# The last attention's keys turned beside the state-space scan, and their norms read as rows from DRAM

## The chip, the cores and the metric

One core of one Trainium2 chip runs the whole program. The core has a matrix engine (TensorE, PE; its weight loads are PEld), a vector engine (VectorE, DVE), a scalar engine (ScalarE, ACT), GpSimd (POOL) and SyncE (SP), which issues nearly all transfers. Each engine takes its own instructions in order and waits for the others only by semaphores. The metric is the device time of one execution in microseconds (us), lower is better.

## The reference

Eight layers stand one after the other on `x` of 4 x 256 tokens with 256 features, each `x = x + layer(layernorm(x))`. Two matter here, the first and the seventh. Shapes are those that reach them (the weights' own setup sizes are others).

```python
# first layer, a selective state-space layer on the context (4 x 256 tokens, 128 features)
x = einsum('bld,ed->bel', ctx, in_proj_w);  x = silu(causal_conv(x, conv_w) + conv_b)
dt_low, Bm, Cm = split(einsum('bdl,ed->bel', x, x_proj_w))       # 8, 16, 16 rows
dt = softplus(dt_proj(dt_low) + dt_proj_b);  A = -exp(A_log)     # 256 x 16
for each token:  state = state * exp(dt * A) + (dt * x) * Bm;  y = sum_n state_n * Cm_n
out = (y + D * x) * silu(z)                                      # z: the normed x

# seventh layer, cross-attention, 16 heads of 128, keys and values from the same context
q = (h @ Wq).reshape(B, 256, 16, 128);  k = (ctx @ Wk)...;  v = (ctx @ Wv)...
q = q * rsqrt(mean(q*q) + 1e-5) * gq
k = k * rsqrt(mean(k*k) + 1e-5) * gk
attn = softmax(einsum('bqhd,bkhd->bhqk', q, k) / sqrt(128))
out = einsum('bhqk,bkhd->bqhd', attn, v).reshape(B, 256, 2048) @ Wo
```

The keys and values of the seventh layer depend on the context alone, so they can be made at any time.

## The kernel before

**The state-space layer (`mamba`).** The 16 states are 16 iterations n. The 256 channels are two halves j of 128 partitions, and a row holds all 1024 tokens. For each state DVE multiplies `dBu` for both halves (L757, L758), scans half 0 (L753), multiplies it by the row of C (L764) and scans half 1 (L753); POOL does the product with C of half 1 (L796). PE spreads a row of B and then a row of C over the partitions into banks 4 and 5 (`spread`, L561) and adds the products into banks 0 to 3 (`add`, L566). ACT makes `exp(dt*A)` (`decay`, L661) and copies the spread row of C out of PSUM (L671). DVE's next state can start when the next row of B is spread (`m_b`), its product with C when that copy is done (`m_c_copied`).

**Keys and values made beside it.** 32 rounds r make the keys and values of the last attention: `kv_round` (PE, 4 products, L503, eight instructions in the trace) into banks 6 and 7, `kv_out` (ACT, L603) into one of four buffers `staged`, and SP stores it to DRAM. 24 rounds stand in the scan: one at the end of every iteration, and a second one ahead of it in each even iteration (`EXTRA`). 16 rounds make keys; `squares` (ACT, L612) sums their squares in the iteration behind. A round waits until the last user of banks 6 and 7 was copied out (`m_kv_copied`). Behind the scan DVE takes the 1/rms of all keys (L195 to L210, `g.k_rs`), between the two output steps `gated_out(0)` and `gated_out(1)` (L770, L773).

**The last attention (`attn4`).** Eight turns t, one for each pair of heads. A turn has 11 slots written out by hand. In slots 0 to 7 a unit (head, sequence) gets its scores (PE, L2717), maximum (DVE, L2868), exponential (ACT, L2804), division (DVE, L2876), transpose of the weights (PE, L2727), its copy (ACT, L2812), the product with V (PE, L2739) and its copy (DVE, L2882), each a slot or more behind the last; the output projection (PE, L2765) follows. The jobs for the next turn stand in the table `JOBS`, by slot, with the PSUM bank: projection of q (PE, L2687, copied by DVE, L2861, squares by ACT, L2784), its transposes (`qt`: PE, L2695, ACT, L2793), and `kt`, the same for k. Before that DVE multiplies a head of k by its 1/rms (L2851, `keys`). A turn -1 has only jobs. POOL takes the 1/rms of q (L107 to L114) from the squares, and DVE needs it (L2886) before the first maximum.

## Time and profile before

| | |
|---|---|
| median of 3 runs | 1496.79 us (1494.49 to 1501.44) |
| profiled execution | 1492.03 us, its span 1490.3 us |
| busy: PE, DVE, ACT, POOL | 87%, 71%, 48%, 14% of the span |
| scan, about 48 to 186 us | iterations of 8.6 us |
| last attention, about 1023 to 1320 us | turns of 36.1 us |

The profile is of one execution. Times in its rows are us from the start of the span. An engine's idle time before an instruction is put down to what released it. PE instructions overlap: eight of one kind start at even distance and the last one's end lies some 0.17 us behind the next one's start. Register, semaphore and branch instructions are not counted as busy.

### The profile page before, as it was taken

To read this page: it belongs to the slowest core of one execution; us is meant where nothing else is said; L and a number is where in the kernel's file an instruction comes from. 1 tells how busy PE (TensorE), PEld (TensorE's weight loads), DVE (VectorE), ACT (ScalarE), POOL (GpSimd) and SP (SyncE) were. 2 spreads that over 40 slices of the span, in tenths; PEclk is the share of its full clock that TensorE was granted. 3 is DMA by queue.
4 is the path that set the end of the run, shared out by engine and by line. 5 is a ranking of instruction groups with operands and counts; after the bars stand their busy time and mean duration, and the time that the engine had idled before them with its cause. 6 is when DMAs were issued, how large, how long until landed. Compare 5 with 4: busy or idle time off the path is not lost.

```text
span 1490.3 us, 20843 instructions
## 1 busy us (share of the span) xinstructions
PE 1302.3 (87%) x6612; PEld 908.7 (61%) x6620; DVE 1052.7 (71%) x2211; ACT 720.0 (48%) x1836; POOL 216.0 (14%) x227
## 2 busy tenths in 40 slices
PE   7788869986998667999998699985999999889998
PEld 4444445652333344676676588984888888774555
DVE  7999987888996787777876623225666666668565
ACT  5788813443775655555544112223666666633111
POOL 0132220000000002211220173111111111201000
PEclk9899979996999769999999699997999999989999
DMA  5122240015420100010004197845322222101230
GB/s 189 72 98 99 85 190 1 1 29 87 78 46 15 70 1 1 1 37 1 36 1 133 56 344 284 305 182 167 106 70 70 70 70 70 35 1 47 77 91 29
DMA packets 77776, 124.61 MB, mean 84 GB/s; under 512 B 44965, under 2 KB 56430, under 8 KB 72352
## 3 DMA queue, kind: packets, MB, share of 16 engines
q1 hardware_dynamic: 75824, 119.37, 24.6%
q0 software_dynamic: 1872, 4.22, 0.7%
q8 instruction: 44, 0.72, 0.2%
q14 instruction: 36, 0.29, 0.1%
HBM read 88.28 MB, written 26.24 MB: 77 GB/s over the span
## 4 chain that ended last, share of the span: by engine, by line
PE 68%; DVE 19%; issue 7%; ACT 4%; DMA 2%; DVEq 1%; SPq 0%; POOL 0%; ACTq 0%; POOLq 0%
PE psum L2397 5%; DVE roomA L753 5%; PE psum L3181 5%; PE psum L873 4%; PE psum L1978 4%; PE psum L2739 4%; PE psum L2687 4%; PE psum L2717 3%; PE psum L2020 3%; PE psum L2765 3%; PE psum L2408 3%; PE psum L3191 3%; PE psum L2010 2%; PE psum L907 2%; DVE roomB L1535 2%
## 5 line engine op out<-in xcount | busy, mean ns | idle before, releaser
L2804 ACT ACTIVATE roomA<-psum,roomA 128x256 f32<-128x256 f32 x128 | 70.9, 559 | 92.7 <-DVE roomA L2870 92.4
L2066 ACT ACTIVATE roomA<-psum,roomA 128x128 f32<-128x128 f32 (+1 forms) x128 | 53.2, 426 | 88.5 <-DVE roomA L2141 88.3
L1535 DVE TENSOR_REDUCE roomB<-psum 128x2 f32<-128x512 f32 x128 | 82.1, 686 | 9.7 <-PE psum L1374 8.4
L2539 DVE SCALAR_TENSOR_TENSOR roomA<-roomA,psum 128x512 f32<-128x512 f32 x23 | 15.9, 689 | 98.6 <-ACT roomA L2444 98.6
L1978 PE MATMUL psum<-own,roomB 128*128 128x512 f32 x160 | 75.0, 594 | 3.4 <-DVE roomA L2133 2.1
L1941 POOL TENSOR_TENSOR roomA<-roomA 128x512 f32<-128x512 f32 x40 | 50.8, 1272 | 176.9 <-DVE roomA L2134 176.9
L3181 PE MATMUL psum<-roomA,roomB 128*112 128x512 f32 (+1 forms) x168 | 74.8, 593 | 0.3 <-DVE roomA L3409 0.3
L2739 PE MATMUL psum<-roomA 128*128 128x256 f32 x256 | 68.3, 389 | 6.0 <-DVE roomA L2882 4.4
L753 DVE TENSOR_TENSOR_SCAN roomA<-roomA 128x1024 f32<-128x1024 f32 x32 | 73.1, 2284 | 0.0
L2717 PE MATMUL psum<-roomA 128*128 128x256 f32 x256 | 65.6, 379 | 1.7 <-ACT roomA L2804 1.7
L873 PE MATMUL psum<-own,roomB 128*128 128x512 f32 x144 | 66.6, 607 | 0.0
L1374 PE MATMUL psum<-roomB,roomA 48*128 48x256 bf16 x256 | 51.9, 301 | 16.7 <-DVE roomB L1535 9.4
L3289 ACT ACTIVATE roomA<-psum 48x512 f32<-48x512 f32 (+1 forms) x32 | 19.0, 594 | 97.8 <-PE psum L3181 97.8
L503 PE MATMUL psum<-roomB,own 128*128 128x256 f32 x256 | 65.3, 403 | 0.0
L503 PEld LDWEIGHTS psum<-roomB,own 128*128 128x128 f32 x256 | 51.6, 203 | 21.5 <-issue 13.0
L2687 PE MATMUL psum<-roomB,own 128*128 128x256 f32 x256 | 62.7, 390 | 1.6 <-DVE own L288 0.8
L566 PE MATMUL psum<-roomA,own 128*128 128x512 f32 x128 | 60.4, 593 | 2.5 <-DVE roomA L764 1.3
L796 POOL TENSOR_TENSOR roomA<-roomA 128x1024 f32<-128x1024 f32 x16 | 37.9, 2366 | 146.4 <-DVE roomA L753 146.4
L2020 PE MATMUL psum<-roomB,roomA 128*128 128x256 f32 x256 | 58.2, 379 | 0.8 <-DVE roomA L2158 0.8
L2450 ACT COPY roomA<-psum 128x256 f32<-128x256 f32 x23 | 8.6, 373 | 100.3 <-PE psum L2408 92.8
L2765 PE MATMUL psum<-roomB,roomA 128*128 128x256 f32 x256 | 56.7, 378 | 0.0
L2687 PEld LDWEIGHTS psum<-roomB,own 128*128 128x128 f32 x256 | 49.9, 196 | 9.6 <-issue 1.1
(526 smaller groups left out, 3331.8 us busy)
## 6 DMA issues: line engine op xcount, KB each, us to landing
roomB<-m_w_dram SPq DMA_DIRECT2D x12, 1536.0 KB
roomA<-m_w_dram SPq DMA_DIRECT2D x11, 1536.0 KB
a_kv_ready<-roomB SPq DMA_DIRECT2D x32, 512.0 KB, 3.1
roomA<-a_kv_ready SPq DMA_DIRECT2D x8, 1024.0 KB, 4.8
roomA<-a_kv_ready SPq DMA_DIRECT2D x16, 512.0 KB, 4.2
roomB<-a_w_dram SPq DMA_DIRECT2D x4, 1280.0 KB, 5.8
roomB<-f_w_dram SPq DMA_DIRECT2D x8, 624.0 KB, 3.9
roomA<-f_c_rows SPq DMA_DIRECT2D x6, 512.0 KB, 3.9
```

The costliest lines, as they stand in the source:

```text
L503: ins = pe.matmul(g.ps[:, at * HALF + i * 2 * P:at * HALF + (i + 1) * 2 * P], g.CT[:, t * P:(t + 1) * P], w_kv[:, place_of[r] // 2 * 2 + k ...
L753: dve.tensor_tensor_scan(h[:, j, :], dA[:, j, :], dBu[j], 0.0, ALU.mult, ALU.add).then_inc(s["m_scanned"], 1)
L873: ins = pe.matmul(g.bank(4 + 2 * (k % 2) + w), w_up[:, kt, e, w * HID:(w + 1) * HID], g.XT[:, kt, half * HALF:(half + 1) * HALF], start=(k ...
L1535: dve.tensor_reduce(maxneg[:, hp // 8, :, m, hp % 8], g.bank(m).rearrange("p (q k) -> p q k", k=S), AX.X, ALU.max, negate=True).then_inc(s ...
L1978: ins = pe.matmul(bank, w, g.XT[:, kt, half * HALF:(half + 1) * HALF], start=(kt == 0), stop=(kt == KD - 1))
L2020: ins = pe.matmul(g.bank(OUT)[:, r * D:(r + 1) * D], OT[:, n % 2, h, r * P:(r + 1) * P], wo[:, h, :], start=(h == 0), stop=(h == HQ - 1))
L2397: ins = pe.matmul(g.bank(4 + 2 * (b % 2) + w)[:, f * P:(f + 1) * P], parts(b)[0][:, kt, at:at + P], xT[:, b % 2, kt, :], start=(kt == 0), ...
L2687: ins = pe.matmul(g.bank(bank)[:, i * 2 * P:(i + 1) * 2 * P], g.XT[:, kt, (2 * j + i) * P:(2 * j + i + 1) * P], w_q[:, kt, :], start=(kt = ...
L2717: ins = pe.matmul(g.bank(2 + n % 2)[:, qt * S:(qt + 1) * S], qT[:, q, i * P:(i + 1) * P], kT[:, q, b * S:(b + 1) * S], start=True, stop=True)
L2739: ins = pe.matmul(g.bank(5, S), V[:, q, (2 * b + kt) * P:(2 * b + kt + 1) * P], PT[:, n % 2, kt, :], start=(kt == 0), stop=(kt == 1))
L2765: ins = pe.matmul(g.bank(OB[k])[:, r * D:(r + 1) * D], OT[:, q, i * P:(i + 1) * P], w_o[:, q, :], start=(q == 0), stop=(q == 1))
L3181: ins = pe.matmul(g.bank(bank, rows=m), w[:, kt, at:at + m], xg[:, n % 2, kt, half * HALF:(half + 1) * HALF], start=(kt == 0), stop=(kt == ...
```

## The change

In `mamba` each keys round is turned in the iteration behind it: `turn_keys` (PE) transposes the eight 128x128 blocks from `staged` into banks 6 and 7, `keys_out` (ACT) copies them to one of two buffers `turned`, and SP stores that instead of `staged`. The list `uses` numbers the rounds and turns in the order in which they take banks 6 and 7. In the attention no k is transposed: DVE multiplies the loaded keys by the gain and by `k_scale`, a row of 1/rms that a broadcast transfer puts on all partitions, into `kT` itself. Those rows come from `a4_scales` in DRAM, written once at the start of the attention from a transpose of `g.k_rs`. `JOBS` loses its four `kt` entries, and `keys` stands in slots 5 and 9 (0 and 2 in turn -1) where it stood in 0 and 5.

```diff
@@ mamba
+    keys_in = [[r for r in rs if kind_of[r] == 0] for rs in in_loop]
+    uses = [("round", r) for r in range(EARLY + MIDDLE)]
+    for n in range(NS):
+        uses += [("turn", r) for r in (keys_in[n - 1] if n else ())] + [("round", r) for r in in_loop[n]]
@@ mamba, tensor
+            before = uses[:uses.index(("round", r))]
+            earlier = [k for k, (what, q) in enumerate(before) if (6 if what == "turn" else pair_of[q]) == at]
             if earlier:
                 pe.wait_ge(s["m_kv_copied"], earlier[-1] + 1)
+        def turn_keys(r):
+            pe.wait_ge(s["m_kv_copied"], uses.index(("turn", r)))
+            for q in range(2):
+                for i in range(4):
+                    ins = pe.transpose(g.bank(6 + q)[:, i * P:(i + 1) * P], staged[:, r % 4, q, i * P:(i + 1) * P], g.ident)
+            ins.then_inc(s["m_kv_psum"], 1)
                 add(1, s["m_added1"])
+            for r in keys_in[n - 1] if n else ():
+                turn_keys(r)
             for r in in_loop[n][:-1]:
                 kv_round(r)
             pe.wait_ge(s["m_hc0"], n + 2)
@@ mamba, scalar
-            for r in in_loop[n - 1] if n else ():
-                if kind_of[r] == 0:
-                    squares(r)
+            for r in keys_in[n - 1] if n else ():
+                squares(r)
+                keys_out(r)
             for r in in_loop[n][:-1]:
                 kv_out(r)
@@ attn4
-    JOBS = {0: (("q", 0, 0),), 1: (("q", 1, 1),), 2: (("q", 2, 6),), 3: (("q", 3, 0),), 4: (("kt", 0, 1),), 5: (("kt", 1, 6),),
-            6: (("qt", 0, 0),), 7: (("qt", 1, 1),), 8: (("kt", 2, 6), ("kt", 3, 0)), 9: (("qt", 2, 1), ("qt", 3, 6))}
+    JOBS = {0: (("q", 0, 0),), 1: (("q", 1, 1),), 2: (("q", 2, 6),), 3: (("q", 3, 0),),
+            5: (("qt", 0, 1),), 6: (("qt", 1, 6),), 8: (("qt", 2, 0),), 9: (("qt", 3, 1),)}
@@ attn4, sync
         def keys(n):
             load(k_in, ready(n, 0), "a4_k_in")
+            load(k_scale.rearrange("p q t -> p (q t)"), scales[bass.ds(n, 1), :].to_broadcast([P, 2 * TOK]), "a4_k_in")
+        sp.wait_ge(s["a4_rows"], 1)
+        sp.wait_ge(s["a4_small"], 16)
+        load(scales.rearrange("n (q i t) -> (n q i) t", q=2, i=NT), rows, "a4_small")
+        sp.wait_ge(s["a4_small"], 32)
         keys(0)
@@ attn4, vector
-            dve.wait_ge(s["a4_k_in"], n * 16 + 16)
-            if units:
-                dve.wait_ge(s["a4_kt_psum"], t * 4 + 2 * q + 2)
-            dve.tensor_tensor(norm_k[:, q], k_in[:, q, :].rearrange("p (i c) -> p i c", c=P),
-                              g.k_rs[:, bass.ds(n * 2 + q, 1), :].rearrange("p a i -> p (a i)").unsqueeze(2).to_broadcast([P, NT, P]),
-                              ALU.mult).then_inc(s["a4_kn"], 1)
+            dve.wait_ge(s["a4_k_in"], n * 32 + 32)
+            dve.scalar_tensor_tensor(kT[:, q, :], k_in[:, q, :], gains[:, 1:2], k_scale[:, q, :], ALU.mult, ALU.mult)\
+               .then_inc(s["a4_kn"], 1)
-                if jobs and slot in (0, 5):
-                    keys(t, slot // 5, units)
+                if jobs and slot in ((5, 9) if units else (0, 2)):
+                    keys(t, int(slot in (2, 9)), units)
```

Two new steps stand ahead of the attention's norm: PE transposes `g.k_rs` and ACT copies it to `rows`. POOL waits once for the last stores before it fills V in the second attention. The line numbers of the changed kernel are some 8 to 31 higher.

On PE, in iteration 2 of the scan (even), these rows stood from the spread of C to the next spread of C: C (L561), `add(1)` (L566), the extra round (L503), the next B (L561), `add(0)` (L566), the last round (L503).

```order
L561 MATMUL psum<-roomA 128x512 x2
L566 MATMUL psum<-roomA,own 128x512 x2
L503 MATMUL psum<-roomB,own 128x256 x4
L561 MATMUL psum<-roomA 128x512 x2
L566 MATMUL psum<-roomA,own 128x512 x2
L503 MATMUL psum<-roomB,own 128x256 x4
```

The same place now (L576 is `spread`, L581 `add`, L511 the round, L519 `turn_keys`):

```order
L576 MATMUL psum<-roomA 128x512 x2
L581 MATMUL psum<-roomA,own 128x512 x2
L519 MATMUL psum<-own,roomB 128x128 x8
L511 MATMUL psum<-roomB,own 128x256 x4
L576 MATMUL psum<-roomA 128x512 x2
L581 MATMUL psum<-roomA,own 128x512 x2
L511 MATMUL psum<-roomB,own 128x256 x4
```

The transposes stand ahead of the extra round, and the spread of the next B stands behind both.

On ACT the same iteration had: the two decays (L661), the copy of the last round of the iteration before (L603), the copy of C (L671), the squares (L612), the copy of the extra round (L603), and the decays.

```order
L661 ACTIVATE roomA<-roomA 128x4x255 x2
L603 COPY roomB<-psum 128x1024
L671 COPY roomA<-psum 128x1024
L612 ACTIVATE roomB,own<-roomB 128x128 x8
L603 COPY roomB<-psum 128x1024
L661 ACTIVATE roomA<-roomA 128x4x255 x2
```

It now has (L685 decay, L620 a round's copy, L695 the copy of C, L636 squares, L627 `keys_out`):

```order
L685 ACTIVATE roomA<-roomA 128x4x255 x2
L620 COPY roomB<-psum 128x1024
L695 COPY roomA<-psum 128x1024
L636 ACTIVATE roomB,own<-roomB 128x128 x8
L627 COPY roomA<-psum 128x1024
L620 COPY roomB<-psum 128x1024
L685 ACTIVATE roomA<-roomA 128x4x255 x2
```

The copy of the transposes stands behind the squares and ahead of the copy of the extra round.

On SP, where the attention starts, behind the loads of the layer before (`m_sums`), the keys (128x2048) and the two halves of V followed:

```order
L2324 DMA roomA<-m_sums 128x2x256 x8
L2614 DMA roomA<-a_kv_ready 128x2048
L2614 DMA roomA<-a_kv_ready 128x1024 x2
L2614 DMA roomB<-a_q_dram 128x512
```

Now:

```order
L2350 DMA roomA<-m_sums 128x2x256 x8
L2642 DMA a_scales<-roomA 128x128
L2642 DMA roomA<-a_kv_ready 128x2048
L2642 DMA roomA<-a_scales 128x2048
L2642 DMA roomA<-a_kv_ready 128x1024 x2
L2642 DMA roomB<-a_q_dram 128x512
```

A store, which SP waits for, stands ahead of the keys, and the load of the scales between the keys and V.

## Rows read from the trace of the kernel before

**Rows 1.** Timeline of DVE, scan, even iteration: start us, duration us, engine, line, instruction [idle before <-releaser]

```profile
100.03 1.22 DVE L757 TENSOR_TENSOR roomA<-roomA,psum 128x1024 f32<-128x1024 f32 x1 [0.40 <-DVE roomA L753]
102.30 2.28 DVE L753 TENSOR_TENSOR_SCAN roomA<-roomA 128x1024 f32<-128x1024 f32 x1
104.80 1.22 DVE L764 TENSOR_TENSOR roomA<-roomA,psum 128x1024 f32<-128x1024 f32 x1 [0.21 <-DVE roomA L753]
...
108.62 1.22 DVE L757 TENSOR_TENSOR roomA<-roomA,psum 128x1024 f32<-128x1024 f32 x1 [0.40 <-DVE roomA L753]
```

**Rows 2.** Timeline of PE, the same iteration

```profile
102.44 0.60 PE L561 MATMUL psum<-roomA 96*128 96x512 bf16 x2 [0.90 <-DVE roomA L758]
...
104.60 1.89 PE L503 MATMUL psum<-roomB,own 128*128 128x256 f32 x8
106.33 0.60 PE L561 MATMUL psum<-roomA 96*128 96x512 bf16 x2
106.76 1.88 PE L566 MATMUL psum<-roomA,own 128*128 128x512 f32 x4
```

**Rows 3.** Timeline of ACT, the same iteration and the next

```profile
103.08 1.01 ACT L671 COPY roomA<-psum 128x1024 f32<-128x1024 f32 x1 [0.49 <-PE psum L561]
...
106.53 1.01 ACT L603 COPY roomB<-psum 128x1024 f32<-128x1024 f32 x1
107.44 2.18 ACT L661 ACTIVATE roomA<-roomA 128x1020 f32<-128x1020 f32 x2
...
111.67 1.01 ACT L671 COPY roomA<-psum 128x1024 f32<-128x1024 f32 x1 [0.25 <-PE psum L561]
```

**Rows 4.** Timeline of DVE and PE behind the last scan

```profile
185.71 1.28 DVE L770 SCALAR_TENSOR_TENSOR roomA<-roomA,roomB,psum 128x1024 f32<-128x1024 f32 x1 [0.22 <-DVE roomA L753]
187.03 2.21 DVE L773 SCALAR_TENSOR_TENSOR roomA<-own,roomA 128x1024 f32<-128x1024 f32 x1
...
193.28 1.22 DVE L773 SCALAR_TENSOR_TENSOR roomA<-own,roomA 128x1024 f32<-128x1024 f32 x1
...
190.03 1.04 PE L592 MATMUL psum<-own,roomA 128*128 128x128 f32 x8
```

**Rows 5.** Windows of the attention: stretch, its us, busy us by engine, PEclk, DMA share, GB/s

```profile
1034.00:1040.00 6.00, 3.67 (x27) 2.65 (x26) 1.82 (x2) 5.91 (x28) 1.67 (x2) 1.00 0.60 195
1113.00:1149.10 36.10, 35.48 (x194) 30.82 (x193) 23.35 (x59) 22.66 (x80) 4.89 (x7) 1.00 0.22 73
1126.34:1134.05 7.71, 7.62 (x47) 6.73 (x46) 7.46 (x20) 6.73 (x25) 3.04 (x2) 1.00 0.12 29
```

**Rows 6.** The chain that ended last, within one turn: start us, us, what

```profile
1131.51 0.44 PE psum L2695 x4
...
1138.90 0.66 PE psum L2695 x4
...
1140.90 0.44 DVE roomA L2882
```

**Rows 7.** Timeline of DVE, the same turn, slot 7

```profile
1134.50 0.69 DVE L2868 TENSOR_REDUCE roomA<-psum 128x2 f32<-128x512 f32 x1 [0.44 <-PE psum L2717]
```

**Rows 8.** Timeline of SP, DVE and PE where the attention starts

```profile
1023.15 1.30 SPq L2614 DMA_DIRECT2D roomA<-a_kv_ready  x3
1030.40 1.22 DVE L2851 TENSOR_TENSOR roomA<-roomA,own 128x1024 f32<-128x1024 f32 x1
...
1043.07 0.18 DVE L2886 TENSOR_SCALAR roomA<-roomA 128x16 f32<-128x16 f32 x1 [6.94 <-POOLq L2839]
...
1046.11 1.02 PE L2717 MATMUL psum<-roomA 128*128 128x256 f32 x4
```

**Rows 9.** DMA issues at the attention's start and in all: operation, count, KB each, us to landing

```profile
roomA<-a_kv_ready SPq DMA_DIRECT2D x2, 1024.0 KB, 4.9
...
roomA<-a_kv_ready SPq DMA_DIRECT2D x2, 512.0 KB, 6.8
...
roomA<-m_steps_dram SPq DMA_DIRECT2D x1, 96.5 KB, 2.0
```

More of the change, by code:

```diff
@@ L462, in mamba @@
     place_of = [(values if kind_of[r] else keys).index(r) for r in range(32)]
+    keys_in = [[r for r in rs if kind_of[r] == 0] for rs in in_loop]
+    assert not keys_in[-1] and min(keys) >= EARLY + MIDDLE
+    uses = [("round", r) for r in range(EARLY + MIDDLE)]
+    for n in range(NS):
+        uses += [("turn", r) for r in (keys_in[n - 1] if n else ())] + [("round", r) for r in in_loop[n]]
     xpad = ra.take(E2, B, S + TAPS - 1)
@@ L470, in mamba @@
     A = ra.take(E2 * NS)
+    turned = ra.take(2, 2, HALF)
     dA, h = e, th
@@ L482, in sync @@
         for r in range(32):
-            sp.wait_ge(s["m_kv_copied"], r + 1)
-            sp.dma_start(g.kv[place_of[r] // 2, kind_of[r], :, :, (place_of[r] % 2) * HALF:(place_of[r] % 2 + 1) * HALF], staged[:, r % 4])\
+            sp.wait_ge(s["m_kv_copied"], uses.index(("round" if kind_of[r] else "turn", r)) + 1)
+            sp.dma_start(g.kv[place_of[r] // 2, kind_of[r], :, :, (place_of[r] % 2) * HALF:(place_of[r] % 2 + 1) * HALF],
+                         staged[:, r % 4] if kind_of[r] else turned[:, place_of[r] % 2])\
               .then_inc(s[f"m_kv_stored{r % 4}"], 16)
@@ L495, in kv_round @@
             at = pair_of[r]
-            earlier = [k for k in range(r) if pair_of[k] == at]
+            before = uses[:uses.index(("round", r))]
+            earlier = [k for k, (what, q) in enumerate(before) if (6 if what == "turn" else pair_of[q]) == at]
             if earlier:
@@ L598, in kv_out @@
         def kv_out(r):
-            act.wait_ge(s["m_kv_psum"], r + 1)
+            act.wait_ge(s["m_kv_psum"], uses.index(("round", r)) + 1)
             if r >= 4:
@@ L603, in kv_out, with keys_out @@
             act.copy(staged[:, r % 4].rearrange("p q (i c) -> p q i c", i=4), src).then_inc(s["m_kv_copied"], 1)
+        def keys_out(r):
+            act.wait_ge(s["m_kv_psum"], uses.index(("turn", r)) + 1)
+            if place_of[r] >= 2:
+                last = keys[place_of[r] - 2]
+                act.wait_ge(s[f"m_kv_stored{last % 4}"], 16 * (last // 4) + 16)
+            act.copy(turned[:, place_of[r] % 2], g.ps[:, 6 * HALF:8 * HALF].rearrange("p (q t) -> p q t", q=2)).then_inc(s["m_kv_copied"], 1)
         def squares(r):
             pair, half = divmod(place_of[r], 2)
-            act.wait_ge(s["m_kv_copied"], r + 1)
+            act.wait_ge(s["m_kv_copied"], uses.index(("round", r)) + 1)
             if place_of[r]:
@@ L1099, in constants @@
         pool.wait_ge(s["f0_made"], 5)
+        for q in range(4):
+            pool.wait_ge(s[f"m_kv_stored{q}"], 8 * 16)
         pool.memset(k.V[:, :, :, HD:], 1.0).then_inc(s["a1_ones"], 1)
@@ L2596, in attn4 @@
     room.at = 0
-    norm_k, raw_q = room.take(2, NT, P), room.take(2, NT, P)
+    raw_q = room.take(2, NT, P)
     kT, qT, V, OT = (room.take(2, TOK) for _ in range(4))
@@ L2603, in attn4 @@
     ta, tb, consts = room.take(2, NT), room.take(2, NT), room.take(3, 2, NT)
-    k_in = room.take(2, TOK)
+    k_in, k_scale = room.take(2, TOK), room.take(2, TOK)
+    rows = room.take(P)
+    scales = g.nc.dram_tensor("a4_scales", (H // 2, 2 * TOK), F32).ap()
     w_q, w_o, gains = g.a4_wq, g.a4_wo, g.a4_gains
-    JOBS = {0: (("q", 0, 0),), 1: (("q", 1, 1),), 2: (("q", 2, 6),), 3: (("q", 3, 0),), 4: (("kt", 0, 1),), 5: (("kt", 1, 6),),
-            6: (("qt", 0, 0),), 7: (("qt", 1, 1),), 8: (("kt", 2, 6), ("kt", 3, 0)), 9: (("qt", 2, 1), ("qt", 3, 6))}
+    JOBS = {0: (("q", 0, 0),), 1: (("q", 1, 1),), 2: (("q", 2, 6),), 3: (("q", 3, 0),),
+            5: (("qt", 0, 1),), 6: (("qt", 1, 6),), 8: (("qt", 2, 0),), 9: (("qt", 3, 1),)}
     SLOTS = 11
@@ L2690, in job @@
             q, half = j // 2, j % 2
-            if what == "kt" and half == 0:
-                pe.wait_ge(s["a4_kn"], n * 2 + q + 1)
-            src = norm_k if what == "kt" else raw_q
             for i in range(4):
-                ins = pe.transpose(g.bank(bank)[:, i * P:(i + 1) * P], src[:, q, 4 * half + i, :], g.ident)
+                ins = pe.transpose(g.bank(bank)[:, i * P:(i + 1) * P], raw_q[:, q, 4 * half + i, :], g.ident)
         ins.then_inc(s[f"a4_{what}_psum"], 1)
@@ L2791, in job @@
                     act.wait_ge(s["a4_scores"], t * 8 + 4 * q + 4)
-                dst, gain = (kT, 1) if what == "kt" else (qT, 0)
-                act.activation(dst[:, q, half * HALF:(half + 1) * HALF], g.bank(bank), ACT.Copy, scale=gains[:, gain:gain + 1])\
+                act.activation(qT[:, q, half * HALF:(half + 1) * HALF], g.bank(bank), ACT.Copy, scale=gains[:, 0:1])\
                    .then_inc(s[f"a4_{what}"], 1)
@@ L2919, in added, with turn_scales, scales_in @@
         dve.sem_inc(s["layer_done"], 1)
+    def turn_scales(pe):
+        pe.transpose(g.bank(0, P), g.k_rs.rearrange("p h i -> p (h i)"), g.ident).then_inc(s["a4_rows_psum"], 1)
+    def scales_in(act):
+        act.wait_ge(s["a4_rows_psum"], 1)
+        act.copy(rows, g.bank(0, P)).then_inc(s["a4_rows"], 1)
     def credits(dve):
+        dve.wait_ge(s["a4_small"], 16)
         dve.sem_inc(s["a4_rs_used"], 1)
```

21 lines of the change are left out of this document (9 added, 12 removed).

## The prediction

> **What bounds the kernel now.** I read the chain that ended last first: DVE carries it through the scan, PE through the last attention. Then the timelines of the two places that the change touches.
>
> *The scan.* DVE's two first multiplies of successive states start at 100.03 and 108.62, 8.59 us apart, and DVE idles only 0.40 and 0.21 us between [rows 1]. DVE is the bound, the others fit around it, and what counts is how late PE and ACT may hand over. PE spreads the next B at 106.33, done at 106.93, 1.69 us before DVE takes it [rows 1, 2]. ACT copies C at 103.08 to 104.09, and DVE needs it at 104.80: 0.71 us to spare [rows 1, 3]; in the odd iteration that follows the copy ends at 112.68, and DVE's product starts at 104.80 + 8.58 = 113.38: 0.70 us to spare.
>
> *The last attention.* One turn is 36.10 us, PE 35.48 of it busy, at granted clock 1.00 [rows 5]. So PE bounds the turn, but not with everything else idle: from 1126.34 to 1134.05 (slots 4 to 6) DVE is busy 7.46 of 7.71 us, without an idle time of its own [rows 5], and only before 1134.50 does it wait, 0.44 us [rows 7].
>
> **The change part by part: the scan.** Added are 16 turnings. One is eight transposes on PE, 1.04 us [rows 4], its place in line 0.87, and one ACT copy of 1024 columns, 1.01 us [rows 3]. The cover is DVE's 8.6 us; a plain count says they fit. They do not fit in an even iteration, because all of it passes through banks 6 and 7 one after the other. I place the new instructions in the rows:
>
> 1. The transposes start where the extra round did, 104.60 [rows 2], and end 105.64.
> 2. Their copy stands on ACT behind the squares, which end at 106.53 (there the extra copy starts now) [rows 3]. It runs to 107.54.
> 3. The extra round waits for that copy: 107.57 instead of 104.60. It takes 1.89 us, 1.73 until the next may start: 109.30.
> 4. Behind it in PE's line is the next B: 109.30 + 0.60 = 109.90, and DVE, ready at 108.62, starts at about 109.94. **Loss 1.32 us.**
> 5. The extra copy runs 109.5 to 110.5, the decays (2.18 us) follow to 112.65. On PE `add(0)` follows B to 111.4, then the last round to 113.3; ACT copies it to 114.35 and then copies C, to 115.35. DVE would take C at 113.38 + 1.32 = 114.70, so it waits until 115.40. **Loss 0.70 us** in the odd iteration, which has no extra round and loses nothing more.
>
> A pair costs 2.03 us. Iteration 0 has no keys behind it; iterations 2 to 13 are six pairs, 12.2 us; iteration 14 gives 1.32. **13.5 us** until iteration 15 starts (at 177.31 before, by the same 8.59 step from 100.03).
>
> Iteration 15 has two keys rounds to turn (those of 14) and PE's `add(0)` behind both turnings. From its start: C copied at 5.4 (step 5's delay), squares 2.4 and copy 1.0 to 8.8; second transposes to 9.7 in line; `add(0)` 1.88 us, to 11.6. `gated_out(0)` needs it. Before it started at 185.71 [rows 4], 8.40 after the iteration's start; now 11.65: 3.25 later. But its second multiply took 2.21 us where the same form later takes 1.22 [rows 4], beside POOL's last product, which now is long done: 0.99 back. The second squares and all else are done before DVE asks. **2.3 us.** The scan's sum: 13.5 + 2.3 = **+15.8 us**. Bounds: every duration is one of a row, so I allow 14 to 17.5.
>
> The stores to DRAM are of the same size and number, an iteration later; the wait that is added to POOL is met long before.
>
> **The turn of the attention.** PE loses 16 transposes, 4 x 0.44 = 1.74 us [rows 6], and a wait of 0.22 on an ACT copy between them (0.66 where others have 0.44). Upper bound of the gain: 1.96 a turn. What of it arrives:
>
> - In the slots, `kt` leaves slots 4, 5 and 8 (twice) and the `qt` of slots 6, 7 and 9 move up: slots 4, 7, 8 and 9 lose 0.44 each. Ahead of slot 7's maximum that is one 0.44, and DVE, whose own work stays (the keys' multiply stays in slot 5; I take its new form at the same 1.22 us, which both forms of 1024 columns have in rows 4 and 8), has just 0.44 of idle there [rows 7]. Played forward from the rows, PE then waits 0.2 us more for DVE's copy of unit 2, and 0.23 arrives.
> - Slots 7 to 9 lose 1.31 + 0.22. There exponentials and copies stand back to back on ACT, and the products of units 4 and 5 wait 0.44 and 0.42 for their copies: 0.67 remains.
> - The keys' multiply of slot 9 stands before DVE's copy that PE already waits for at 1140.90 [rows 6]. Between that copy and the one before are 1.75 us of PE work (two groups of four transposes, one product), DVE needs 0.42 + 1.22: it just fits, and the 0.44 stays.
>
> I take **0.9 us a turn**, seven turns have jobs beside units: **-6.3 us**. Bounds: 0.4 (more of the softmax chain) to 1.96, so -2.8 to -13.7.
>
> **The attention's start.** The keys' load was issued at 1023.15, landed 4.9 us later, and DVE took them at 1030.40, when the norm let it [rows 8, 9]. Now a store of 64 KB stands first and SP waits for it; the 96.5 KB load has 2.0 us to landing [rows 9], so I take 2.0. Behind it the scales, 1 MB, stand where V's two halves stood, and those had 6.8 us from issue to landing, the last of them 7.2 after the first issue. 1023.15 + 2.0 + 7.2 = 1032.4: the multiply starts 2.0 us late. Back come 0.6 us, since ACT has no `kt` copy ahead of the last squares. All that follows (q copies, squares, POOL's root, L2886 at 1043.07 [rows 8]) comes some 1.4 us later; PE's third scores at 1046.11 had 0.5 us of room after the exponential. **+1.0 us.** Bounds: -1.2 if the loads are hidden (then the ACT saving counts), +3.5 if a row read by all 128 partitions is slow.
>
> **Sum.** +15.8 - 6.3 + 1.0 = **+10.5 us**, on the profiled 1492.0: 1502.5. That execution was 4.8 us below the median of the runs, 1496.8, so the median becomes 1507.3; I give **1507**.
>
> **A rule weighed.** In the stretch from 1034 to 1040 PE did little but transposes, 3.67 of 6.00 us busy, and the clock granted was 1.00 [rows 5]. The Trainium skill, "TensorE: Matmul & The Clock Gate", Part 4 (PE-mode transpose), says that transposes do not count as busy for the clock. By that rule the scan's PE, a larger share of it transposes and with a wait of 2 us in every second iteration, could fall to the granted clock 0.5, which is 1.2 GHz; the row speaks against it.
>
> **The rivals.**
>
> - *Full PE saving* (13 in 100). The attention is PE-bound to the end and gives 1.96 a turn: 15.8 - 13.7 + 1.0 = +3.1, 1500. For it: PE 35.48 of 36.10. Against: DVE without idle in slots 4 to 6.
> - *The extra round does not hold the spread* (9 in 100, half of them with the full saving). The one point that decides is step 4: B has 1.69 us to spare and loses 2.97. If transposes and copy cost 1.3 us less than placed, the pairs cost nothing, and +2.3 + 1.0 remain: with -6.3, 1494; with -13.7, **1486, faster**. Against: all the durations are of rows.
> - *The start is worse and the turns give little* (13 in 100): 15.8 + 3.5 - 2.8 = +16.5, 1513. The scales' broadcast is the one transfer with no like in the trace.
> - *PE's clock falls in the scan* (2 in 100). A pair needs some 15.4 us of PE (four spreads at 0.43, four adds and three rounds at 1.73, two turnings at 0.87, less fill) of its 17.2 now; at half clock near 31. Seven times 12: +80 us.
> - *As worked out* (63 in 100): 1507, its own range 1503 to 1511.
>
> The range, 8 in 10: **1500 to 1514**, from the full saving to the bad start. What a measurement here can tell from no change is about 0.5%, 7.5 us, so slower begins at 1504.3. Slower: the forecast less a twelfth, the bad start, the clock: **0.73**. Same: the full saving, half of the second rival and the rest of the forecast: **0.22**. Faster: **0.05**.
>
> **What the changed profile would show.** Step 3: in even iterations PE's extra round starts near 7.5 us after DVE's first multiply (4.57 now). Step 4: DVE idles about 1.7 us before that multiply every second time, released by PE's spread; step 5: 0.9 us before its product with C, released by ACT's copy. Tail: the first multiply of the output (L770 before) starts some 2.8 us behind the last scan, not 0.2. Attention: turns of 35.2 us, PE with new waits of 0.3 to 0.5 us in slots 6 to 8. Start: the first keys' multiply near 2 us later relative to the norm. It is wrong if the scan's iterations stay at 8.6 us, or the turns are at 34.2.

## The result, and the profile after

The change makes the kernel 0.8% slower, little but clear of the noise: 1509.70 us (median of 6 runs, 1508.19 to 1514.77) against 1498.93 us (6 runs), ratio 1.0083, 95% interval 1.0060 to 1.0106. By the ratio that is +12.4 us, 9 to 16; the two medians by themselves are 10.8 us apart. The prediction was 1507 in 1500 to 1514, or +10.5 us.

The profiled executions stand further apart, 1514.77 to 1492.03: before's lay 7 us below its median, after's 5 above. So I compare section by section, on starts of rows. `rs_now` is DVE's first instruction of a turn, which takes the 1/rms of q.

| section | before | after | difference | predicted |
|---|---|---|---|---|
| scan, first multiply to that of iteration 15 | 128.83 | 141.82 | +13.0 | +13.5 |
| from there to the layer's first add on DVE | 17.94 | 21.52 | +3.6 | +2.3 |
| first feed-forward layer (not touched): from that add to the next layer's norm (L251) | 130.36 | 132.17 | +1.8 | 0 |
| attention: last add of the layer ahead to the first `rs_now` (L2886, now L2909) | 20.5 | 23.6 | +3.1 | +1.0 |
| seven steps from `rs_now` to `rs_now` | 253.81 | 247.84 | -6.0 | -6.3 |

The rest of the profiled difference, some 7 us, lies in layers that the change does not touch. They differ as much between two executions of one program: a kernel below that is the kernel before up to 1022 us has one such layer 8.5 us longer.

*Scan.* Timeline of the changed kernel, iterations 6 (even) and 7, which are those of the rows before (start, length, line; idle time ahead and its releaser in brackets). DVE first, answering to [rows 1]:

```profile
104.74 1.22 DVE L781 TENSOR_TENSOR roomA<-roomA,psum 128x1024 f32<-128x1024 f32 x1 [0.40 <-DVE roomA L777]
114.56 1.22 DVE L781 TENSOR_TENSOR roomA<-roomA,psum 128x1024 f32<-128x1024 f32 x1 [1.63 <-PE psum L576]
120.05 1.22 DVE L788 TENSOR_TENSOR roomA<-roomA,psum 128x1024 f32<-128x1024 f32 x1 [0.94 <-ACT roomA L695]
123.87 1.22 DVE L781 TENSOR_TENSOR roomA<-roomA,psum 128x1024 f32<-128x1024 f32 x1 [0.40 <-DVE roomA L777]
```

PE there, answering to [rows 2] (L519 transposes, L511 a round, L576 a spread):

```profile
109.31 1.04 PE L519 MATMUL psum<-own,roomB 128*128 128x128 f32 x8
112.09 1.99 PE L511 MATMUL psum<-roomB,own 128*128 128x256 f32 x8 [1.75 <-ACT roomA L627]
113.92 0.60 PE L576 MATMUL psum<-roomA 96*128 96x512 bf16 x2
```

ACT there, the turned copy and the extra round's, answering to [rows 3]:

```profile
111.04 0.99 ACT L627 COPY roomA<-psum 128x1024 f32<-128x1024 f32 x1
114.12 1.01 ACT L620 COPY roomB<-psum 128x1024 f32<-128x1024 f32 x1 [2.08 <-PE psum L511]
```

Steps 1 to 5 in order: transposes end 5.6 us after the first multiply, their copy starts behind the squares at 6.3, the extra round at 7.35 (predicted 7.5), DVE waits 1.63 us for B (predicted 1.7) and in the odd iteration 0.94 for C (predicted 0.9; 0.21 of it stands in every iteration). The iterations last 9.82 and 9.31 us, a pair 19.13; before, 17.17.

*Tail.* PE and DVE of iteration 15, answering to [rows 4], then the windows there (us, busy time and count of each engine; granted clock third from the end):

```profile
199.74 1.55 PE L519 MATMUL psum<-own,roomB 128*128 128x128 f32 x8 [2.22 <-ACT roomA L627]
201.09 3.15 PE L581 MATMUL psum<-roomA,own 128*128 128x512 f32 x4
```

```profile
204.28 1.28 DVE L794 SCALAR_TENSOR_TENSOR roomA<-roomA,roomB,psum 128x1024 f32<-128x1024 f32 x1 [4.28 <-PE psum L581]
205.59 1.22 DVE L797 SCALAR_TENSOR_TENSOR roomA<-own,roomA 128x1024 f32<-128x1024 f32 x1
```

```profile
199.00:201.00 2.00, 1.26 (x8) 1.26 (x9) 1.00 (x1) 2.00 (x11) 0.69 (x1) 0.81 0.08 25
201.00:203.00 2.00, 2.00 (x5) 0.96 (x4) 0.00 (x0) 1.93 (x9) 1.67 (x1) 0.50 0.64 246
```

The second turning waits 2.22 us for the first copy; the granted clock falls to 0.50 (1.2 GHz), and `add(0)`, 1.88 us elsewhere, takes 3.15. The second output step is back at 1.22 us, as the prediction had it. Three kernels below have the same scan: two of them read the same tail, +3.6, and the third keeps the clock and reads +1.9.

*Start of the attention.* DVE, answering to [rows 8], and the transfers' issues (KB each, us to landing), answering to [rows 9]:

```profile
1055.05 0.69 DVE L288 COPY own<-psum 128x512 f32<-128x512 f32 x1 [3.90 <-PE psum L304]
1057.92 1.28 DVE L2875 SCALAR_TENSOR_TENSOR roomA<-roomA,roomB 128x1024 f32<-128x1024 f32 x1 [2.18 <-DMA roomA<-a_scales]
1059.12 0.68 DVE L2884 COPY roomA<-psum 128x512 f32<-128x512 f32 x1
1070.64 0.18 DVE L2909 TENSOR_SCALAR roomA<-roomA 128x16 f32<-128x16 f32 x1 [6.76 <-POOLq L2865]
```

```profile
roomA<-a_kv_ready SPq DMA_DIRECT2D x1, 1024.0 KB, 4.8
roomA<-a_scales SPq DMA_DIRECT2D x1, 1024.0 KB, 8.2
```

DVE starts the multiply 0.14 us behind the landing of the scales. ACT's first squares of q and, four instructions later, those of the second copy of q:

```profile
1059.89 0.31 ACT L2811 ACTIVATE roomA<-roomA 128x128 f32<-128x128 f32 x1 [4.70 <-DVE roomA L2884]
1061.63 0.31 ACT L2811 ACTIVATE roomA<-roomA 128x128 f32<-128x128 f32 x1 [0.46 <-DVE roomA L2884]
```

Seven kernels below keep this start. In their executions and this one the section is 22.3 to 24.1 us, 1.8 to 3.6 longer than before, so +3.1 is one draw out of these. From the start of the multiply to `rs_now` it is 12.7 us in all eight and in the kernel before, so what differs is when the scales land.

*Turns.* One turn's window, answering to [rows 5], and PE's waits in it, which answer to [rows 6]:

```profile
1139.59:1174.59 35.00, 34.03 (x178) 29.14 (x177) 23.39 (x59) 20.61 (x76) 5.13 (x7) 1.00 0.29 105
```

```profile
1159.74 1.13 PE L2766 MATMUL psum<-roomA 128*128 128x256 f32 x4 [0.23 <-ACT roomA L2838]
1161.92 1.12 PE L2766 MATMUL psum<-roomA 128*128 128x256 f32 x4 [0.18 <-ACT roomA L2838]
1165.30 1.13 PE L2766 MATMUL psum<-roomA 128*128 128x256 f32 x4 [0.52 <-DVE roomA L2905]
```

A steady turn is 35.00 us instead of 36.10: 1.10 arrives. The first step gives 1.46, but the seventh is 0.99 us longer than before. There one pair of DVE's divisions takes 4.41 us, the others 0.61 to 0.69:

```profile
1301.58 4.41 DVE L2899 TENSOR_SCALAR roomA<-roomA 128x256 f32<-128x256 f32 x2
```

The stall is there in the kernel before too (4.32 us), and with the attention of either version; the seventh step varies from 36.8 to 40.9 us over all kernels. It is no doing of the change.

### The profile page after: what moved, and what is told of

It reads as the page before. It is cut to its first block, busy times and chain, and to the rows that moved or that the text cites. A ratio compares the mean times of both kernels' runs of the same rounds, so it can differ in the third digit from the quotient of the medians.

```text
span 1513.0 us, 20755 instructions
## 1 busy us (share of the span) xinstructions
PE 1320.2 (87%) x6621; PEld 916.3 (61%) x6621; DVE 1051.4 (69%) x2211; ACT 716.6 (47%) x1821; POOL 217.8 (14%) x227
## 4 chain that ended last, share of the span: by engine, by line
PE 62%; DVE 18%; ACT 7%; issue 7%; DMA 3%; POOL 1%; SPq 0%; DVEq 0%; ACTq 0%; POOLq 0%
PE psum L3212 5%; PE psum L2423 4%; PE psum L2004 4%; PE psum L897 4%; PE psum L2046 3%; PE psum L2792 3%; PE psum L2717 3%; PE psum L3222 3%; PE psum L2434 2%; PE psum L2766 2%; PE psum L2744 2%; PE psum L511 2%; PE psum L2036 2%; PE psum L1400 2%; DVE roomB L1561 2%
## 5 line engine op out<-in xcount | busy, mean ns | idle before, releaser
L1561 DVE TENSOR_REDUCE roomB<-psum 128x2 f32<-128x512 f32 x128 | 82.1, 686 | 14.0 <-PE psum L1400 12.7
L511 PE MATMUL psum<-roomB,own 128*128 128x256 f32 x256 | 65.4, 403 | 13.4 <-ACT roomA L627 12.2
L511 PEld LDWEIGHTS psum<-roomB,own 128*128 128x128 f32 x256 | 50.2, 200 | 33.2 <-ACT roomA L627 16.5
L581 PE MATMUL psum<-roomA,own 128*128 128x512 f32 x128 | 61.5, 603 | 0.0
L2046 PE MATMUL psum<-roomB,roomA 128*128 128x256 f32 x256 | 58.2, 379 | 0.8 <-DVE roomA L2184 0.8
L2891 DVE TENSOR_REDUCE roomA<-psum 128x2 f32<-128x512 f32 x64 | 44.1, 689 | 21.1 <-PE psum L2744 19.4
L2717 PEld LDWEIGHTS psum<-roomB,own 128*128 128x128 f32 x256 | 51.2, 201 | 12.4 <-DVE roomA L2884 2.5
```

Of the source, the lines that this page charges most:

```text
L511: ins = pe.matmul(g.ps[:, at * HALF + i * 2 * P:at * HALF + (i + 1) * 2 * P], g.CT[:, t * P:(t + 1) * P], w_kv[:, place_of[r] // 2 * 2 + k ...
L1561: dve.tensor_reduce(maxneg[:, hp // 8, :, m, hp % 8], g.bank(m).rearrange("p (q k) -> p q k", k=S), AX.X, ALU.max, negate=True).then_inc(s ...
L2046: ins = pe.matmul(g.bank(OUT)[:, r * D:(r + 1) * D], OT[:, n % 2, h, r * P:(r + 1) * P], wo[:, h, :], start=(h == 0), stop=(h == HQ - 1))
L2717: ins = pe.matmul(g.bank(bank)[:, i * 2 * P:(i + 1) * 2 * P], g.XT[:, kt, (2 * j + i) * P:(2 * j + i + 1) * P], w_q[:, kt, :], start=(kt = ...
```

## The experiments

Twelve kernels, each timed beside the kernel before, whose medians there are 1498.0 to 1498.7 us. A difference in us that stands beside a ratio is worked out from it; differences of medians can be some us off from that. The sections are read as in the table above, each from one execution.

**The two halves apart.** Each kernel has one half of the change, here in words:

```
 scan_alone:       turn_keys, keys_out, uses, turned, store of turned; attn4 as before
 attention_alone:  JOBS, keys, k_scale, a4_scales as after; mamba as before
```

> The turning beside the scan as in the changed kernel, the attention as before, which transposes the keys once more: its output is another one, its work is that of before. It separates the scan's part from the rest. My theory: the scan's section costs what the changed trace shows, +16.6 us (prediction: +15.8), and nothing else moves: 1498.9 + 16 = about 1515, slower by 1.1%. Rival A, the loss is mostly the attention's and the low clock in other layers: the scan's section still reads +16, but the whole is under +12. Iterations 17.2 us a pair before, 19.1 here.

> The attention of the changed kernel alone, over keys that the state-space layer stores unturned: its output is another one, its work is that of the changed kernel. My theory: turns of 35.0 us instead of 36.1, the last turn with jobs 1 us longer than the rest, a start 2.7 us later: 1498.9 - 5.6 + 2.7 = 1496, that is 3 us or 0.2% faster. Rival B, the turn is bound by PE alone and could give the full 1.96 us: 1498.9 - 13.7 + 2.7 = 1488.

Measured: scan alone 1519.26 us, ratio 1.0123 (1.0089 to 1.0156), +18 us; its scan section reads +16.6, the feed-forward layer behind it +1.9. Attention alone 1497.13, ratio 0.9963 (0.9936 to 0.9990), -5.5 us; steady turns of 35.01, start +3.3. By the ratios the parts add up to +12.9, and the whole change gave +12.4. The medians are further off (+21.3 and -0.9 against +10.8), so the sum is tested to some us only; the traces' sections, +16.6, +3.3 and -7.3, are the firmer evidence. Rival A falls. Rival B (1488, ratio 0.9933) lies just outside the interval, and the turns in the trace refute it.

**The place of the turned copy on ACT, and of the transposes on PE.**

```diff
             for r in keys_in[n - 1] if n else ():
-                squares(r)
                 keys_out(r)
+                squares(r)
```

```diff
+            for r in keys_in[n - 1] if n else ():       # the second kernel alone
+                turn_keys(r)
             if n:
                 pe.wait_ge(s["m_hc1"], n + 1)
                 add(1, s["m_added1"])
-            for r in keys_in[n - 1] if n else ():
-                turn_keys(r)
```

> In the changed kernel ACT copies the turned block before it sums the squares of the same round, not behind them. My theory (the copy's place behind the squares holds the extra round, and that the next B): in even iterations the extra round starts 2.4 us earlier until the transposes' own end limits it, so of the loss of 1.32 about 0.5 stays; in odd ones ACT's queue is as long as before and the 0.70 stays. Pairs of 18.4 us instead of 19.1, and the tail 1.4 less: 7 us less than the changed kernel, about 1502.5. Rival C, the cost is the added work of PE or ACT or a lower clock, wherever it stands: no change, 1509.7.

> As the one before, and PE turns the keys ahead of the sum add(1) instead of behind it, in the time in which it waits for POOL's product. My theory: the bank is free before the extra round comes up, no iteration is longer than 8.6 us, the loss of 13.5 us is gone, and only the tail of iteration 15 stays at about +2.4 us: 15 us less than the changed kernel, about 1495, with all the added work still in it. Rival C (the work itself): no change, 1509.7. Rival D (PE's order can't win back more than ACT's): 1502.5, as the one before.

Measured: 1503.31 us, ratio 1.0039 (1.0022 to 1.0057), and 1500.48, ratio 1.0006 (0.9982 to 1.0031). In DVE's timeline of the first kernel the wait for B fell from 1.63 to 0.99 us, and that for C stayed at 0.94, as expected:

```profile
113.11 1.22 DVE L781 TENSOR_TENSOR roomA<-roomA,psum 128x1024 f32<-128x1024 f32 x1 [0.99 <-PE psum L576]
118.60 1.22 DVE L788 TENSOR_TENSOR roomA<-roomA,psum 128x1024 f32<-128x1024 f32 x1 [0.94 <-ACT roomA L695]
```

In the second kernel DVE no longer waits for B, and for C at most 0.35 us (0.21 before); iterations last 8.58 to 8.73 us:

```profile
118.61 1.22 DVE L781 TENSOR_TENSOR roomA<-roomA,psum 128x1024 f32<-128x1024 f32 x1 [0.40 <-DVE roomA L777]
127.20 1.22 DVE L781 TENSOR_TENSOR roomA<-roomA,psum 128x1024 f32<-128x1024 f32 x1 [0.40 <-DVE roomA L777]
```

With all the added work still in it, the scan up to iteration 15 is 129.47 us, 0.6 over before. So 12.4 of the 13.0 us were the order on two engines. From iteration 1 to 14 the clock is 1.00 in both kernels, as in the changed one. Rivals C and D fall. The scan's section is 14.6 us shorter than the changed kernel's, as expected; the medians differ by 9 and the ratios by 11.5 us, which their intervals cover.

**C ahead of the last round's copy**, on top of the first kernel above, whose lines for `keys_out` are not shown again.

```diff
+            if n and n % 2 == 0:
-            if n:
                 kv_out(in_loop[n - 1][-1])
             act.wait_ge(s["m_c"], n + 1)
             act.wait_ge(s["m_hc1"], n + 1)
             act.copy(c_all, g.ps[:, 4 * HALF:6 * HALF]).then_inc(s["m_c_copied"], 1)
+            if n % 2:
+                kv_out(in_loop[n - 1][-1])
```

> Turned copies ahead of the squares, and in odd iterations ACT copies the row of C ahead of the last round's keys and values. It takes step 5 alone: DVE's product with C in odd iterations waits 0.2 instead of 0.94 us; the last round's copy is 1 us later, so that the turning behind it and the next spread of B take back about 0.5 in even iterations. Pairs of 18.1 instead of 18.5, about 1 to 2 us less in the scan's section than with the copies first alone. Rival: the product with C waits for the spread of C or for POOL, not for ACT's queue: 0.9 us of wait stays.

Measured: 1503.70 us, ratio 1.0029 (1.0012 to 1.0045), its scan section 2.4 us shorter than with the copies first alone, pairs of 18.02. In odd iterations DVE waits 0.32 us for C (0.21 of it stands in all iterations), and ACT waits 1.07 us for PE's spread before it copies: step 5 was ACT's queue. The last round's copy is later in exchange, and in even iterations DVE waits 0.64 for C and no longer than elsewhere for B. The gain of the section isn't visible in the medians.

**Without the transposes.**

```diff
         def turn_keys(r):
             pe.wait_ge(s["m_kv_copied"], uses.index(("turn", r)))
-            for q in range(2):
-                for i in range(4):
-                    ins = pe.transpose(g.bank(6 + q)[:, i * P:(i + 1) * P], staged[...], g.ident)
-            ins.then_inc(s["m_kv_psum"], 1)
+            pe.sem_inc(s["m_kv_psum"], 1)
```

> The changed kernel without its 128 transposes of keys beside the scan: PE signals at once, ACT's copies stay where they are and copy what the banks hold (the output is another one). My theory (the copy behind the squares holds the extra round, and PE's transposes end long before it): not one iteration gets shorter, pairs of 19.1 us, the tail up to 0.9 less: about 1509. Rival F, PE's own added work of 0.87 us a turning is what costs: the extra round starts 0.87 earlier in even iterations, 6 us less or more, 1503.

Measured: 1519.78 us (4 runs), ratio 1.0124 (1.0083 to 1.0164): with less work, slower than the changed kernel, 10 us by the medians and 6 by the ratios, whose intervals overlap. The traces settle it: the scan's section is 10.4 us longer than the changed kernel's. PE's rows there:

```profile
108.87 1.89 PE L511 MATMUL psum<-roomB,own 128*128 128x256 f32 x8
116.60 3.54 PE L511 MATMUL psum<-roomB,own 128*128 128x256 f32 x8 [2.62 <-ACT roomA L624]
```

The extra round starts 7.35 us after DVE's first multiply, just as in the changed kernel. So the transposes' own time was not in that chain, the copy was: rival F falls. But my 1509 missed what the idle time does. PE waits 2.62 us where it waited 1.75, the round takes 3.54 us instead of 1.99, and DVE waits 3.17 us for B. All seven even iterations have this wait with a slower round behind it. The windows around it:

```profile
112.00:116.00 4.00, 1.98 (x6) 0.64 (x4) 3.79 (x3) 3.70 (x18) 0.00 (x0) 1.00 0.01 2
116.00:120.00 4.00, 3.40 (x9) 2.66 (x10) 1.43 (x1) 0.55 (x1) 2.26 (x1) 0.57 0.33 131
```

I took the transposes away once more, from the kernel with the copies first.

> Without the 128 transposes beside the scan (the output is another one), and with the turned copies ahead of the squares. Taking the same transposes away with the copies behind the squares made the kernel slower by 10 us, where I read a wait of PE of 2.62 us and behind it a granted clock of 0.57 (rounds of 3.54 us instead of 1.89). If that wait is the cause, the clock stays at 1.00 in the scan here, since the copy no longer makes PE wait for over 2 us: pairs of 17.3 us, 7 us less than with the transposes in the same order (1503.3), about 1496. Rival G, what is slow is something else in a scan with no transposes: rounds of 3.5 us here too, over 1510.

Measured: 1495.14 us, ratio 0.9979 (0.9961 to 0.9996). In iteration 6 the extra round starts 5.03 us behind DVE's first multiply (6.71 with the transposes, in the same order), PE waits 0.30 us for it, and it runs at full speed:

```profile
104.70 1.99 PE L511 MATMUL psum<-roomB,own 128*128 128x256 f32 x8 [0.30 <-ACT roomA L624]
```

The clock is 1.00 in every stretch of 10 us from 100 to 180; one of them:

```profile
110.00:120.00 10.00, 7.70 (x26) 3.93 (x25) 9.39 (x7) 8.36 (x23) 2.91 (x2) 1.00 0.18 71
```

All iterations are 8.59 us. Rival G falls; the wait ahead of the round is what slowed it. Here the transposes do count: with the copy early, they are what holds the extra round.

**The multiply of the keys in the attention.**

```diff
-                if jobs and slot in ((5, 9) if units else (0, 2)):
-                    keys(t, int(slot in (2, 9)), units)
+                if jobs and slot in (5, 9):                          # keys_behind_q
+                    keys(t, int(slot == 9), units)
```

```diff
             dve.wait_ge(s["a4_k_in"], n * 32 + 32)
+            if units:                                                # no_multiply
+                return dve.sem_inc(s["a4_kn"], 1)
```

> In the turn ahead of the attention's first, DVE multiplies the keys behind its copies of q instead of ahead of them (slots 5 and 9 in place of 0 and 2). My theory (the scales land 8.2 us after issue and hold DVE's queue, so the squares of q and POOL's root are late): the first copy of q moves up from 2.6 us behind its place to where PE lets it, the root is done 3 to 3.5 us earlier, and the start is then shorter than before by 0.5: 3 us less than the changed kernel, about 1506.5. Rival E, the start is late because of PE (its lower granted clock there, 0.7, at the projections of q): at most the two multiplies' 1.3 us come back.

> The changed kernel without DVE's two multiplies of keys (1.28 us each) in the seven turns that have units beside jobs; the keys of the first pair of heads are used in all (the output is another one). PE's instructions are the same. My theory (DVE without idle time in slots 4 to 6 hands on the softmax chain late): turns of 34.55 instead of 35.01 us, 3 us in all: 1506.5. Rival B, PE alone bounds the turn: 35.01 stays, 1509.7. The bound of PE's own work would be 34.1.

Measured: 1505.75 us, ratio 1.0036 (1.0016 to 1.0056), and 1507.47, ratio 1.0056 (1.0037 to 1.0075). In the first, the way from the norm's last copy (L288) to `rs_now` is 12.28 us; it was 15.59 in the changed kernel and 13.28 before:

```profile
1048.63 0.69 DVE L288 COPY own<-psum 128x512 f32<-128x512 f32 x1 [2.92 <-PE psum L304]
1053.75 2.47 DVE L2875 SCALAR_TENSOR_TENSOR roomA<-roomA,roomB 128x1024 f32<-128x1024 f32 x2
1060.91 0.17 DVE L2909 TENSOR_SCALAR roomA<-roomA 128x16 f32<-128x16 f32 x1 [4.69 <-POOLq L2865]
```

That is 3.3 us, and counted from the end of the layer ahead it is 4.3 (19.3 against 23.6), so rival E (1.3 at most) falls. In the changed kernel PE does wait 2.07 us for the late copy of q, and the clock is 0.50 from 1061 to 1063, but that is not on the way: in three of the eight executions with this start these products run at full clock, and `rs_now` comes 12.7 us behind the multiply just the same. In the second kernel the steady turns are 34.84 us, neither my 34.55 nor the rival's 35.01. One window, and the waits of PE in it:

```profile
1133.63:1168.46 34.83, 33.85 (x178) 29.10 (x177) 21.03 (x58) 20.48 (x76) 4.23 (x7) 1.00 0.29 105
```

```profile
1155.79 1.12 PE L2766 MATMUL psum<-roomA 128*128 128x256 f32 x4 [0.38 <-ACT roomA L2838]
1159.17 1.13 PE L2766 MATMUL psum<-roomA 128*128 128x256 f32 x4 [0.52 <-DVE roomA L2907]
```

DVE's multiplies cost 0.17 us a turn. The last wait, 0.52 us, is the same with them and without: the last two units' products follow each other through one bank and DVE's copy of it, with nothing left for PE to do between.

**Versions of the whole computation.** The first, `all_three`, has the edits of copy first and turn first, the multiplies behind q ahead of the first turn and in slots 8 and 9 in the others. The next two, `all_four` and `tail_copy_first`, change iteration 15 besides, where two rounds of keys are turned (`turns` are those rounds; the first of them is still turned ahead of `add(1)`; those lines are not shown):

```diff
             add(0, s["m_added0"])
+            for r in turns[1:]:                                      # all_four, tail_copy_first
+                turn_keys(r)
             kv_round(in_loop[n][-1])
```

```diff
+            for r in turns[:1]:                                      # all_four; tail_copy_first
+                keys_out(r)                                          # has copy, squares, copy, squares
+            for r in turns:
+                squares(r)
+            for r in turns[1:]:
+                keys_out(r)
```

> Everything that the runs so far point to, the computation whole: turned copies ahead of the squares, transposes ahead of add(1), the keys' multiply behind the copies of q ahead of the first turn, and in slots 8 and 9 in place of 5 and 9 in the others. Against the kernel before, by the theory: scan's section +2, first feed-forward layer +1.8 (its lower clock stays as in all kernels that turn beside the scan), start of the attention -0.5, turns 34.7 instead of 36.1 us, 7 times: -9.8. Sum -6.5: 1491.5, 0.4% faster. Rival (the turns keep 35.0, the start +2.7): -3.5 + 2.7, 1498 to 1500.

> The version with three edits, and in iteration 15 the second turning on PE behind add(0) in place of ahead of add(1), its copy on ACT behind both squares; the computation is whole. My theory of the tail (DVE's first output step waits 2.36 us for add(0), which stands behind two turnings): that wait goes, DVE may then wait up to 0.8 us for the squares; scan's section 1.5 us shorter, so level with that of before to 0.5 us. About 1493.5, 0.4% faster than before. Rival H (the second turning only moves the wait behind the first output step, to PE's last round): 1495.3, as with three.

> As the version with four edits, but ACT copies the second turned block of iteration 15 ahead of the second squares, not behind both; the computation is whole. With the copy behind them PE waited 2.57 us, its granted clock fell to 0.5 and DVE's second output step waited 2.65 us for the last add(1). My theory: the copy ends 1.7 us earlier, PE waits under 1 us, the clock stays at 1.00, and DVE is held by the squares only: the scan's section 1.8 us shorter than with four edits, 0.9 shorter than with three. About 1494.5, 0.3% faster than before. Rival: the clock falls there all the same, and nothing is gained: 1495.4.

Measured: 1495.33 us, ratio 0.9970 (0.9947 to 0.9994); 1495.39, ratio 0.9972 (0.9955 to 0.9989); 1492.84, ratio 0.9950 (0.9928 to 0.9972). The first was expected at 1491.5 and reads scan section +2.0, feed-forward layer +2.1, start -0.8, steady turns 34.93: slots 8 and 9 brought 0.07 us a turn, not 0.3. The second came out at its rival H's time, with the wait moved as H had it, while its feed-forward layer is 2.1 us shorter than the first's, which hides what the scan's end lost. DVE's wait of 2.36 us for `add(0)` went, but PE stood 2.57 us before its last round and DVE then 2.65 before its second output step, where the section is 1.2 us longer than the first's:

```profile
189.54 2.72 PE L511 MATMUL psum<-roomB,own 128*128 128x256 f32 x8 [2.57 <-ACT roomA L630]
```

```profile
195.07 1.28 DVE L801 SCALAR_TENSOR_TENSOR roomA<-roomA,roomB,psum 128x1024 f32<-128x1024 f32 x1 [2.65 <-PE psum L581]
```

The third's PE waits 1.10 us at full clock, and DVE only 0.67 for the squares:

```profile
188.91 1.99 PE L511 MATMUL psum<-roomB,own 128*128 128x256 f32 x8 [1.10 <-ACT roomA L630]
```

```profile
191.23 0.23 DVE L195 TENSOR_SCALAR roomB<-own 128x128 f32<-128x128 f32 x1 [0.67 <-ACT roomB L639]
```

Its section is 0.4 us shorter than the first's (0.9 expected) and 1.6 shorter than the second's (1.8). Its rival, a low clock there all the same, falls. It is the fastest version, 0.5% below the kernel before; the 2.5 us between the medians of the first and the third are more than the traces account for, and within the intervals.

## Why the prediction was right, point by point

- **Steps 1 to 5 of the scan** stand in the trace to 0.2 us. That the order is the cause, on ACT first and then on PE, and not the work, is shown from three sides: the order alone takes 12.4 us back, the transposes taken away alone win nothing, and with and without them the round starts 7.35 us into the iteration. +13.5 was +13.0: an even iteration lost 1.24, not 1.32.
- **The tail**, +2.3, was mis-sized: +3.6 in the profiled execution. Its mechanism holds, PE's `add(0)` behind two turnings. What I left out is the granted clock. The kernel without the keys' multiply, whose scan is the same, has the same wait of PE at clock 1.00, `add(0)` at 1.88 us and a tail of +1.9. So the low clock is 1.7 of the 3.6, and the rest is 0.4 below the sum as it was worked out.
- **The start**, +1.0, was mis-sized too: +3.1. Counted from the end of the layer ahead the multiply starts at 10.9 us instead of 7.8; the prediction's own sum gives 9.8. The store took 1.6 us, 0.4 less than the 2.0 allowed, but the scales landed 8.2 us after issue, where 6.8 had been taken: 1.1 us late in all. The 0.6 that I let come back did not. ACT's copy of `kt` is gone, but the second multiply now stands in slot 2, ahead of DVE's second copy of q, and ACT waits 0.46 us for that copy. The last 0.4, the room at the third scores, lies behind the section. PE's low clock there has no part in it. With the multiplies behind q the section is 19.3 to 20.0 us in all four kernels, shorter than before. Why the scales land at 6.9 us in three executions and at 8.2 to 8.4 in nine stays open.
- **The turns**, -6.3, came to -6.0, from 0.9 a turn where 1.10 arrived and a seventh turn that gave nothing in this execution. With the attention alone it was -7.3. The upper bound of 1.96 did not come because three waits stand where one stood, as the prediction placed them; but DVE's multiplies have a share of 0.17 in it, where their run had been expected to show 0.46.
- **The first feed-forward layer** was in no step. It is not touched and took 1.8 us more. In the 50 us behind the layer's first add the mean granted clock was 0.80 before and 0.76 after. In one stretch of 2 us there, 15 us behind that add, it was 0.93 before and 0.50 after, two windows:

```profile
210.00:212.00 2.00, 2.00 (x19) 2.00 (x18) 1.93 (x3) 0.00 (x0) 1.87 (x3) 0.93 0.69 222
```

```profile
227.30:229.30 2.00, 2.00 (x11) 2.00 (x11) 1.93 (x3) 0.00 (x0) 1.87 (x3) 0.50 0.78 249
```

  In eleven of the twelve kernels with a changed scan the layer is 1.7 to 2.2 us longer, and the mean clock of those 50 us is 0.74 to 0.77. In the twelfth, `all_four`, it is level with before, at 0.83, and so it is with the attention changed alone, at 0.80. So the loss goes with the clock. What at the scan's end decides the clock stays open: no run tests it.
- **PE's clock in the scan** (2 in 100, +80 us) did not fall in the changed kernel: 1.00 from iteration 1 until late in iteration 15 (iteration 0 has a low clock before and after). Its condition was placed wrongly: not the transposes bring the clock down, an idle PE does, and where it did so, without the transposes, the scan up to iteration 15 took 12.0 us more, not 80, because only what stands behind the wait is slow.
- **The other rivals.** The full saving of 1.96 a turn did not come (1.10). The extra round does hold the spread. Of the bad start and weak turns the first half nearly came, +3.1 of the +3.5 allowed, the second did not.
- **The sum**, +10.5: the sections of the table add up to +15.5 in the two profiled executions. Of the 5.0 between, 3.4 are the two mis-sized terms, 1.8 the layer behind the scan and 0.3 the turns, less 0.5 in the scan. The ratio says +12.4 (9 to 16), the medians +10.8. The mechanism of the largest term, the scan, is shown; that the total came within 2 us of the ratio is partly luck: the profiled sections miss the forecast by 5.0 us, nearly all of it one way, and the interval holds both 10.5 and 15.5.

## What to carry to other kernels

Work that passes through one PSUM bank pair costs by its place in the queues, not by its length: 16 turnings of 0.87 us on PE and 1.01 on ACT cost 0.6 us of scan once the copy that frees the banks stood ahead of the squares, which nobody waits for, and the transposes in a wait that PE had anyway, and cost 13 us behind it. When an edit adds a round trip PE, ACT, PE, list what the copy stands behind, and put waits for a slow third engine behind the new work. The same holds for an instruction that waits for a load: the multiply at the head of DVE's queue made all of the start as late as its scales. Price a new wait of PE of 2 us or more, as they stand here, with the instructions behind it at half clock too: taking work away ahead of such a wait can cost more than the work did.

## What the runs showed of the hardware

- **The granted clock can fall behind waits of PE.** The wait of 1.75 us in the scan left it at 1.00, in all seven even iterations of the four kernels that have it. The wait of 2.62 us (without transposes) had 0.50 to 0.78 in the 2 us behind it all seven times, with rounds of up to 3.8 us instead of 1.99, and that of 2.57 us (iteration 15, `all_four`) a round of 2.72. The wait of 2.22 us, at one place of one program order, had 0.50 behind it in three executions and 1.00 in the fourth. Length alone does not decide: at the attention's start waits of 2.07 to 4.15 us had eight products in 3.2 to 3.6 us behind them in five executions, and one of 2.87 us had them in 2.00; at the end of the scan without transposes a wait of 3.49 us had 1.00 behind it, and in the kernel before one of the same length 0.52. The Trainium skill, "TensorE: Matmul & The Clock Gate", Part 1, says of the clock's rise that its moment varies from run to run; what varies here is the fall.
- **Transposes keep the clock up.** With 1.04 us of them ahead of the wait the scan's clock is 1.00, without them 0.57 in the stretch behind. The same page of the Trainium skill, Part 4 (PE-mode transpose), says that transposes don't count as busy for the clock. By that rule PE would be idle equally long in both kernels, 0.87 + 1.75 against 2.62 us, and they should not differ; they do, by 12.0 us up to iteration 15, so for these fp32 transposes the measurement decides against it.
- **A row read by all 128 partitions** (8 KB to 1 MB), behind another load of 1 MB, landed 8.2 to 8.4 us after issue at the attention's start in nine executions and 6.9 in three, with nothing between, and 6.8 us in the median of all eight of the changed kernel. The load of 1 MB ahead of it took 4.7 to 4.9. In that place the two halves of V (1 MB together) had 6.8 at the start and 4.2 in the median before. No run tells the reading of one row apart from the size of the single load.
- **The fused multiply** with a scalar of each partition takes 1.28 us for 1024 columns, the plain one 1.22.
